# Decoder layer on one NeuronCore: the attention step's two transpositions, second diagonals and output projection in another order

## The chip, the core and the metric

One Trainium2 chip, one NeuronCore. The metric is device time in microseconds (us) of one execution of the whole kernel; lower is better. TensorE (PE, with its weight loads as PEld), VectorE (DVE), ScalarE (ACT), GpSimd (POOL) and SyncE (SP, which issues the DMAs) each run a stream of their own, in order, and meet at semaphores.

## The reference, cut

Four sequences of 512 tokens, width 512. A gated slot attention of 16 heads (key 64, value 128, 64 slots), a grouped-query cross attention without weights, and a ternary-like feed-forward of 1408, each followed by a residual add and a layernorm. The change lies in the first part alone:

```python
q, k, v = heads(x @ Wq, 64), heads(x @ Wk, 64), heads(x @ Wv, 128)
s = clip(heads(x @ Ws, 64), -32, 32)
z = cumlogsumexp(s);  p = exp(s - z);  g = exp(z_before - z)
hk = hk * g + k p^T;   ok = q/8 . hk          # scan over tokens, first pass
pv = softmax(ok)                              # over the 64 slots
hv = hv * g + p v^T;   o = pv . hv            # scan over tokens, second pass
gate = x @ Wg
o = o * rsqrt(mean(o^2) + eps) * g_norm_weight * silu(gate)
x = layernorm(x + o @ Wo)
```

## The kernel before

Attention runs in 32 steps (NSTEP), one for each pair of heads (8 pairs, `p`) and each sequence (4, `j`): step `n` = 4p + j. Both scans are done in chunks of 64 tokens (CHUNKS = 8): inside a chunk by a masked product ("diagonal"), across chunks by running sums of the chunks' states. Every projection is made with three matmuls for one (`mm3`, L61 to L63: low by high, high by low, high by high, in fp32r), for precision.

A step does the second half of pair-and-sequence n and the projections for n + 1, and is software pipelined by hand: the order of the calls in each engine's `step` is the order in which that engine works. The calls that matter here, on PE, in their order before the change:

- `key_scores` (L1202), the projections S and K of step n + 1 (12 x 2 matmuls of 512 columns), `key_states` (L1218), `slots` (L1271), `states` (L1239), `slots_from_states` (L1282).
- projection V0 (VG in the code: v and gate of 128 tokens, 12 matmuls), then **the slots' transposition** (`transpose4(okb, ... okn ...)`, L1129) which waits for okn_ready.
- V1, V2, then **the weights' transposition** (`transpose4(tb, ... pv ...)`, L1129 as well), which waits for pv_ready.
- V3, then wT_ready, the **second diagonals** (`diagonals`, L1228) and `values_from_states` (L1295).
- projection Q, the output projection of step n - 1 (`project_out`, four tiles of 6 matmuls, L61 to L63 with a_wo in their names), and `values` (L1305).

Up to step 28 (`LATE_OUT`) the output projection stands there; in the last three steps it stands elsewhere, and these keep their order. Step 0 has no output projection, so 28 steps (1 to 28) do.

The output projection's four tiles use two PSUM banks (`out_banks`: okb and tb, tile t in bank t % 2). Tile 2 waits until DVE has added tile 0 to acc, tile 3 until tile 1 is added (`wait(pe, added, 4 * (n - 1) + t - 1)` in `project_out`). The adds are `add_out` on DVE (L1968), each behind its tile (`wo_done`).

The two projection banks `pj` alternate: a projection waits until the one two before it has been read, V and gate groups by `gating` on DVE (L1880), which follows the copy of v (L1642) and the tanh (L1644) on ACT.

DVE's order around the change, before: `gating` V0, `slot_maxima` (L1989), `less_maxima` (L1994), `gating` V1, `slot_sum` (L2000), `scaled_weights` (L2004, waits for the weights' transposition and gives wT), `gating` V2, `slot_reciprocals` (L2008), `running_z` (L1888, a scan of the next step's exponentials into rz, which must not overwrite rz before `scaled_weights` has read it), `low_turned` (L1960), `mask_diagonal_blocks` (L1917, waits for the second diagonals and for ACT's `rows_of_keys`), `gating` V3, `inverse_z` (L1894 and L1895, two reciprocals of 128 x 256), the four adds, `gated_output` (L2017).

ACT's order: V0's copies, the exponential (L1710), V1's copies, `rows_of_e` (L1664, waits for a DMA), V2's copies, `high_turned` (L1658, waits for a DMA), `rows_of_keys` (L1670, waits for a DMA), V3's copies, the copy of Q (L1623), sums of squares (L1686).

SP sends e, the outputs and the keys to DRAM in 32-row blocks and fetches them back turned (`put_e`, `put_og`, `put_keys`, `get_e`, `get_og`, `get_keys`), then loads weights. POOL does the norm's factor and the splits of weights. Neither has a changed line.

Of the kernel before, what the change touches and what calls it, by code (L numbers as in the profile page):

```python
# [142 lines left out]
def layer_program(nc, x, ctx_in, Wq, Wk, Wv, Wg, Ws, Wo, gw, gate_w, up_w, down_w, gate_s, up_s, down_s, out,  # L143
# [6 lines left out]
    with ExitStack() as ctx:  # L150
# [10 lines left out]
        def sem(name):  # L161
            return ctx.enter_context(nc.semaphore("a_" + name))
# [102 lines left out]
        ok_done = sem("ok_done")  # L265
        pvT_done = sem("pvT_done")
        o_done = sem("o_done")
        e_done = sem("e_done")

        queries_kept = sem("queries_kept")  # L270
# [61 lines left out]
        def at(n, k):  # L332

            return isinstance(n, int) and n == k
# [714 lines left out]
        def _(pe):  # L1049
# [237 lines left out]
            def values_from_states(n):  # L1287

                ob = value_banks(n)
                if LATE_OUT < n < NSTEP - 1:  # L1290
                    pe.wait_ge(added, 4 * n)
                for c in range(1, CHUNKS):
                    i, r = c // 2, c % 2
                    for h in range(2):
                        pe.matmul(ob[h][HALF[r ^ h], i * P:(i + 1) * P], wT[HALF[h], c * CHUNK:(c + 1) * CHUNK],  # L1295
                                  state[HALF[h], c - 1, :], start=(c == 1 or c == 2), stop=False, skip_group_check=True)

            def values(n, j):

# [20 lines left out]
            def step(n, p, j, first):  # L1320
                b1, pair1 = (j + 1) % B, p if j < B - 1 else p + 1

                def next_project(*groups):
                    for i in groups:
                        project(n + 1, i, b1, pair1)

                into = n == NSTEP - 2
                key_scores(n)
                next_project(S, K)
                key_states(n)  # L1330
                slots(n)
                states(n, j)
                slots_from_states(n)
                next_project(VG)
                pe.wait_ge(okn_ready, n + 1)
                transpose4(okb, [okn[:, t * P:(t + 1) * P] for t in range(TT)]).then_inc(ok_done, 1)
                pair0 = p if j else p - 1
                if at(n, 0):
                    pe.wait_ge(state_ready, CHUNKS - 1)
                    transpose_x(2, range(KT))  # L1340
                if at(n, 1):
                    transpose_x(3, (0, 1))
                next_project(VG + 1)
                if into:
                    transpose_operands(0, 0, 0)
                    transpose_operands(0, 0, 1)
                next_project(VG + 2)
                if into:
                    pe.wait_ge(opsT_ready, 1)
                    transpose_operands(0, 0, 2)  # L1350
                pe.wait_ge(pv_ready, n + 1)
                pe.wait_ge(state_ready, (CHUNKS - 1) * (n + 1))
                transpose4(tb, [pv[:, 2 * t:2 * t + 2, :].rearrange("p h m -> p (h m)") for t in range(TT)])\
                    .then_inc(pvT_done, 1)
                if at(n, 1):
                    transpose_x(3, (2, 3))
                if into:
                    pe.wait_ge(opsT_ready, 2)
                    transpose_operands(0, 0, 3)
                next_project(VG + 3)  # L1360
                if into:
                    pe.wait_ge(opsT_ready, 3)
                    transpose_operands(0, 0, 4)
                    pe.wait_ge(wT_ready, n + 1)
                    max_pair(0, 0)
                if n > LATE_OUT:
                    project_out(n, pair0, (0, 1))
                    if into:
                        max_pair(0, 1)
                    project_out(n, pair0, (2, 3))  # L1370
                pe.wait_ge(wT_ready, n + 1)
                if at(n, 0) or at(n, 1):
                    pe.wait_ge(xlo_ready, (n + 3) * KT)
                if into:
                    pe.wait_ge(opsT_ready, TILES)
                    max_pair(0, 2)
                diagonals(n)
                values_from_states(n)
                if into:
                    max_pair(0, 3)  # L1380
                next_project(Q)
                if not first and n <= LATE_OUT:
                    project_out(n, pair0, (0, 1, 2, 3))
                if into:
                    max_pair(0, 4)
                pe.wait_ge(proj_done, PROJ * (n + 2))
                values(n, j)
# [200 lines left out]
        def _(act):  # L1588
# [109 lines left out]
            def step(n, p, j, first):  # L1698
                b1 = (j + 1) % B

                def next_proj(*groups):
                    for i in groups:
                        copy_proj(n + 1, i, b1)

                if not first:
                    square_sums(n - 1, 0)
                into = n == NSTEP - 2
                next_proj(S, K, VG)
                act.wait_ge(sub_ready, n + 1)
                nc.scalar.activation(pv, pv, ACT.Exp, scale=QK_SCALE).then_inc(pv_ready, 1)  # L1710
                if at(n, 0):
                    high_x(2)
                if at(n, 1):
                    high_x(3, (0, 1))
                next_proj(VG + 1)
                if into:
                    copy_keys(0, 0)
                    copy_queries(0, 0, 1)
                rows_of_e(n + 1)
                next_proj(VG + 2)  # L1720
                if at(n, 1):
                    high_x(3, (2, 3))
                if into:
                    copy_queries(0, 0, 2)
                    copy_queries(0, 0, 3)
                if not first:
                    high_turned(n)
                rows_of_keys(n + 1)
                next_proj(VG + 3)
                if into:  # L1730
                    copy_queries(0, 0, 4)
                next_proj(Q)
                square_sums(n, 1)
                place_sums(n)
# [97 lines left out]
        def _(dve):  # L1832
# [189 lines left out]
            def step(n, p, j, first):  # L2022
                b1 = (j + 1) % B
                norm_now = at(p, PAIRS - 1) and j > 0
                into = n == NSTEP - 2
                late = n <= LATE_OUT
                mask_scores(n)
                if not first:
                    gated_output(n - 1, (j - 1) % B, 1)
                clip(n + 1, b1)  # L2030
                turn_e(n + 1)
                running_key_states(n)
                if not first:
                    turn_output(n)
                normalised_slots(n)
                turn_keys(n + 1)
                running_states(n)
                gating(n + 1, VG, b1)
                slot_maxima(n)
                less_maxima(n)  # L2040
                if at(n, 0):
                    low_x(2)
                if at(n, 1):
                    low_x(3, (0, 1))
                gating(n + 1, VG + 1, b1)
                slot_sum(n)
                scaled_weights(n)
                gating(n + 1, VG + 2, b1)
                slot_reciprocals(n)
                if at(n, 1):  # L2050
                    low_x(3, (2, 3))
                running_z(n + 1)
                if not first:
                    low_turned(n)
                if late:
                    mask_diagonal_blocks(n)
                gating(n + 1, VG + 3, b1)
                if into:
                    reduce_max(0, 0, 0)
                if not first and not late:  # L2060
                    add_out(n, (j - 1) % B, (0, 1))
                if into:
                    reduce_max(0, 0, 1)
                if not first and not late:
                    add_out(n, (j - 1) % B, (2, 3))
                if into:
                    reduce_max(0, 0, 2)
                if not late:
                    mask_diagonal_blocks(n)
                if norm_now and not into:  # L2070
                    statistics(n, j - 1)
                if into:
                    reduce_max(0, 0, 3)
                    reduce_max(0, 0, 4)
                if norm_now and not into:
                    norm.apply(dve, j - 1, j - 1, j - 1)
                inverse_z(n + 1)
                if not first and late:
                    add_out(n, (j - 1) % B, (0, 1, 2, 3))
                gated_output(n, j, 0)  # L2080
# [245 lines left out]
```

## Time and profile before

| what | value |
|---|---|
| median of 3 runs | 1848.08 us (1846.91 to 1848.42) |
| the profiled execution's own time | 1847.07 us |
| its span on the core | 1845.0 us |
| attention's steps 2 to 28 begin | 94.66 to 925.50 us |
| PE busy | 1806.2 us, 98% |
| DVE busy | 1346.9 us, 73% |
| ACT busy | 734.9 us, 40% |
| POOL busy | 571.9 us, 31% |

The page gives busy shares over the whole span, and in 40 slices. PE's matmuls are pipelined, so its records overlap; how long a stretch takes is read best from the start of one group of matmuls to the start of the next. A view by windows gives busy time and the granted clock of a stretch; the view of waits says who waited for whom; the timeline lists instructions by their start, with the idle time before one and what ended it in square brackets.

### The profile page before, as it was taken

The numbers are of one execution on the slowest core, as the hardware profiler recorded it, in microseconds if no ns is written. First come the engines' busy times: TensorE is split into PE (matmuls) and PEld (weight loads), VectorE is DVE, ScalarE is ACT, GpSimd is POOL, SyncE is SP. The second block draws the span as 40 slices with busy tenths as digits, with TensorE's granted clock in tenths as the row PEclk, the third lists the DMA queues.
The fourth block names the chain that finished last, engine by engine and source line by source line (L and its number), as shares of the span: only waits on it lengthen the run. The fifth ranks groups of instructions, "written<-read, shape, count | busy, mean of one in ns | idle before, by whom it ended". The sixth has DMA issues, their size and how long they took to land.

```text
span 1845.0 us, 39065 instructions
## 1 busy us (share of the span) xinstructions
PE 1806.2 (98%) x15728; PEld 1327.9 (72%) x15728; DVE 1346.9 (73%) x2459; ACT 734.9 (40%) x1853; POOL 571.9 (31%) x595
## 2 busy tenths in 40 slices
PE   9999999999999999999998899999999999999998
PEld 7888888888888888888886654444434488888886
DVE  4777677777777677677776789999999665555556
ACT  3323332322323332223322238888888722222223
POOL 3050341333332412503322242444423133323322
PEclk9999999999999999999998889999999999999999
DMA  4324232422333142323212101111111211111112
GB/s 155 97 57 117 68 111 59 110 81 70 87 90 101 51 123 64 92 82 87 81 47 60 44 20 28 26 25 28 28 29 22 28 17 31 22 26 27 18 18 91
DMA packets 191267, 111.63 MB, mean 61 GB/s; under 512 B 96624, under 2 KB 170864, under 8 KB 191088
## 3 DMA queue, kind: packets, MB, share of 16 engines
q1 hardware_dynamic: 191088, 109.14, 22.6%
q8 instruction: 125, 2.05, 0.5%
q14 instruction: 54, 0.44, 0.1%
HBM read 64.77 MB, written 36.18 MB: 55 GB/s over the span
## 4 chain that ended last, share of the span: by engine, by line
PE 91%; DVE 3%; ACT 3%; POOL 1%; issue 1%; DMA 0%; SPq 0%; POOLq 0%; DVEq 0%; ACTq 0%
PE a_ps L61 21%; PE a_ps L63 20%; PE a_ps L62 20%; PE a_ps L1113 6%; PE a_ps L1075 5%; PE a_ps L1097 3%; PE a_ps L1129 2%; PE a_ps L1057 2%; ACT x_prob L1774 2%; PE a_ps L1305 2%; PE a_ps L1282 1%; PE a_ps L1239 1%; PE a_ps L1295 1%; PE a_ps L1228 1%; PE a_ps L1120 1%; DVE a_raw_qks L1838 1%
## 5 line engine op out<-in xcount | busy, mean ns | idle before, releaser
L1838 DVE TENSOR_REDUCE a_raw_qks<-a_ps 128x1 f32<-128x512 f32 x512 | 320.8, 681 | 19.2 <-PE a_ps L1075 18.5
L1774 ACT ACTIVATE x_prob<-a_ps 128x512 f32<-128x512 f32 x512 | 280.0, 608 | 62.9 <-PE a_ps L1097 61.4
L61 PE MATMUL a_ps<-a_vg_hi,a_xT_lo 128*128 128x512 f32 x512 | 209.2, 409 | 0.0
L63 PE MATMUL a_ps<-a_vg_hi,a_xT_hi 128*128 128x512 f32 x512 | 200.7, 392 | 0.0
L62 PE MATMUL a_ps<-a_vg_lo,a_xT_hi 128*128 128x512 f32 x512 | 199.5, 390 | 0.0
L893 POOL TENSOR_TENSOR a_f<-a_rs 128x8 f32<-128x8 f32 x32 | 6.4, 201 | 606.4 <-ACT a_flat L1686 606.4
L61 PE MATMUL a_ps<-a_xT_hi,a_qks_lo 128*128 128x512 f32 x384 | 157.1, 409 | 0.4 <-DVE a_xT_lo L1869 0.4
L1968 DVE TENSOR_TENSOR acc<-acc,a_ps 128x512 f32<-128x512 f32 x128 | 87.8, 687 | 89.1 <-PE a_ps L63 88.6
L62 PE MATMUL a_ps<-a_xT_lo,a_qks_hi 128*128 128x512 f32 x384 | 150.7, 392 | 0.0
L63 PE MATMUL a_ps<-a_xT_hi,a_qks_hi 128*128 128x512 f32 x384 | 149.9, 390 | 0.0
L1075 PE MATMUL a_ps<-a_xT_lo,a_xT_hi 64*128 64x512 f32 x384 | 143.3, 462 | 3.1 <-DVE a_raw_qks L1838 2.5
L1097 PE MATMUL a_ps<-a_xT_hi,a_xT_lo 64*128 64x512 f32 x384 | 140.8, 452 | 0.6 <-ACT x_prob L1774 0.5
L1686 ACT ACTIVATE a_flat<-a_ps 128x128 bf16<-128x128 f32 x256 | 67.4, 278 | 182.2 <-PE a_ps L1305 174.8
L61 PE MATMUL a_ps<-a_xT_hi,f_gu_lo 128*128 128x512 f32 x352 | 137.4, 390 | 0.8 <-POOL f_gu_lo L992 0.8
L1113 PE MATMUL a_ps<-x_prob,x_values 128*32 128x512 f32 x1024 | 137.0, 608 | 0.0
L63 PE MATMUL a_ps<-a_xT_hi,f_gu_hi 128*128 128x512 f32 x352 | 137.0, 389 | 0.0
L62 PE MATMUL a_ps<-f_xT_lo,f_gu_hi 128*128 128x512 f32 x352 | 137.0, 389 | 0.0
L1075 PEld LDWEIGHTS a_ps<-a_xT_lo,a_xT_hi 64*128 64x128 f32 x384 | 61.1, 188 | 98.5 <-issue 39.6
L1642 ACT COPY a_v<-a_ps 128x256 f32<-128x256 f32 x128 | 47.1, 368 | 201.2 <-PE a_ps L63 201.0
L2197 DVE TENSOR_TENSOR acc<-acc,a_ps 128x512 f32<-128x512 f32 x172 | 114.0, 684 | 0.0
L63 PEld LDWEIGHTS a_ps<-a_vg_hi,a_xT_hi 128*128 128x128 f32 x512 | 96.1, 188 | 21.5
L61 PE MATMUL a_ps<-a_wo_hi,a_oT_lo 128*128 128x512 f32 x256 | 101.8, 398 | 8.6 <-DVE a_oT_lo L1960 7.0
(201 smaller groups left out, 4055.0 us busy)
## 6 DMA issues: line engine op xcount, KB each, us to landing
a_og_blocks<-a_og_turn SPq DMA_DIRECT2D x120, 128.0 KB, 2.4
a_og_turn<-a_og_blocks SPq DMA_DIRECT2D x30, 512.0 KB, 4.0
a_e_blocks<-a_e_turn SPq DMA_DIRECT2D x124, 64.0 KB, 1.8
a_key_blocks<-a_causal SPq DMA_DIRECT2D x124, 64.0 KB, 1.8
a_e_turn<-a_e_blocks SPq DMA_DIRECT2D x31, 256.0 KB, 2.9
a_causal<-a_key_blocks SPq DMA_DIRECT2D x31, 256.0 KB, 4.1
a_raw_vg<-in_L_attn_Wv_dram SPq DMA_DIRECT2D x8, 512.0 KB, 6.7
a_raw_vg<-in_L_attn_Wg_dram SPq DMA_DIRECT2D x8, 512.0 KB, 7.8
```

The lines of the kernel that those rows point to most:

```text
L61: pe.matmul(out, w_lo, x_hi, start=start, stop=False)
L62: pe.matmul(out, w_hi, x_lo, start=False, stop=False)
L63: return pe.matmul(out, w_hi, x_hi, start=False, stop=stop)
L1075: pe.matmul(max_bank(u, q, i, par), qs[q][HALF[par], tile, st * P:(st + 1) * P], ks[q][(tile // 2) ^ par][HALF[par], :], start=True, stop= ...
L1097: pe.matmul(score_bank(q, s, par), ks[q][g ^ par][HALF[par], t * P:(t + 1) * P], qs[q][HALF[par], 2 * g + pair, :], start=True, stop=True) ...
L1113: mm = pe.matmul(avb[32 * i:32 * (i + 1), :], cv[:, q, t, g, :], prob[i % 2][:, (s + i // 2) % 4, :], start=(t == 0), stop=(t == TT - 1))
L1642: nc.scalar.copy(v[:, b % 2, i - VG, :], bank[:, 0:2 * DV]).then_inc(v_ready, 1)
L1686: sq = nc.scalar.activation(squares[:, g, 0:DV], ob[half][:, t * P:(t + 1) * P], ACT.Square, scale=DV ** -0.5, accum_out=crossed_sums[:, t ...
L1774: nc.scalar.activation(prob[par][:, s % 4, :], score_bank(q, s, par), ACT.Exp, scale=X_SCALE).then_inc(exp_done[par], 1)
L1838: nc.vector.tensor_reduce(nm[:, q % 2, i % 4, par, i // 4:i // 4 + 1], max_bank(u, q, i, par), AX.X, ALU.max, negate=True).then_inc(max_re ...
L1968: nc.vector.tensor_tensor(a, a, out_banks(n)[t % 2], ALU.add).then_inc(added, 1)
L2197: nc.vector.tensor_tensor(a, a, down_bank(t), ALU.add).then_inc(f_added, 1)
```

## The change

In the steps up to LATE_OUT:

- PE: V1 is put in front of the slots' transposition, and V3 in front of the weights' transposition. Q goes in front of the second diagonals and `values_from_states`, so that these stand right in front of the output projection.
- PE: in front of `values`, the wait for the projections' end becomes a wait for the output projection's first tile (step 0: for a new semaphore vals_started, which `values_from_states` raises).
- PE, steps 0 and 1: the transpositions of x and the wait for xlo_ready move along.
- ACT: V1's copies go in front of the exponential. For all steps, the copies of x of step 1 (tiles 2 and 3) go behind V3's.
- DVE: `gating` V1 goes in front of `slot_maxima`; `low_turned` directly behind `gating` V2 (in all steps); `gating` V3 and then `scaled_weights` behind it; `running_z` and `mask_diagonal_blocks` follow. `slot_reciprocals` stands behind `slot_sum` in all steps. `inverse_z` and the adds keep their place behind all that.

```diff
@@ PE @@
                 for c in range(1, CHUNKS):
                     i, r = c // 2, c % 2
                     for h in range(2):
-                        pe.matmul(ob[h][HALF[r ^ h], i * P:(i + 1) * P], wT[HALF[h], c * CHUNK:(c + 1) * CHUNK],
-                                  state[HALF[h], c - 1, :], start=(c == 1 or c == 2), stop=False, skip_group_check=True)
+                        mm = pe.matmul(ob[h][HALF[r ^ h], i * P:(i + 1) * P], wT[HALF[h], c * CHUNK:(c + 1) * CHUNK],
+                                       state[HALF[h], c - 1, :], start=(c == 1 or c == 2), stop=False,
+                                       skip_group_check=True)
+                if n == 0:
+                    mm.then_inc(vals_started, 1)
...
                 slots_from_states(n)
+                pair0 = p if j else p - 1
+                if n <= LATE_OUT:
+                    next_project(VG, VG + 1)
+                    pe.wait_ge(okn_ready, n + 1)
+                    transpose4(okb, [okn[:, t * P:(t + 1) * P] for t in range(TT)]).then_inc(ok_done, 1)
+                    if at(n, 0):
+                        pe.wait_ge(state_ready, CHUNKS - 1)
+                        transpose_x(2, range(KT))
+                    if at(n, 1):
+                        transpose_x(3, (0, 1))
+                    next_project(VG + 2, VG + 3)
+                    pe.wait_ge(pv_ready, n + 1)
+                    pe.wait_ge(state_ready, (CHUNKS - 1) * (n + 1))
+                    transpose4(tb, [pv[:, 2 * t:2 * t + 2, :].rearrange("p h m -> p (h m)") for t in range(TT)])\
+                        .then_inc(pvT_done, 1)
+                    if at(n, 1):
+                        transpose_x(3, (2, 3))
+                    next_project(Q)
+                    pe.wait_ge(wT_ready, n + 1)
+                    if at(n, 0) or at(n, 1):
+                        pe.wait_ge(xlo_ready, (n + 3) * KT)
+                    diagonals(n)
+                    values_from_states(n)
+                    if not first:
+                        project_out(n, pair0, (0, 1, 2, 3))
+                        pe.wait_ge(wo_done, 4 * (n - 1) + 1)
+                    else:
+                        pe.wait_ge(vals_started, 1)
+                    values(n, j)
+                    return
                 next_project(VG)
                 pe.wait_ge(okn_ready, n + 1)
...
                 next_project(Q)
-                if not first and n <= LATE_OUT:
-                    project_out(n, pair0, (0, 1, 2, 3))
                 if into:
@@ ACT @@
                 next_proj(S, K, VG)
+                if n <= LATE_OUT:
+                    next_proj(VG + 1)
                 act.wait_ge(sub_ready, n + 1)
                 nc.scalar.activation(pv, pv, ACT.Exp, scale=QK_SCALE).then_inc(pv_ready, 1)
...
-                next_proj(VG + 1)
+                if n > LATE_OUT:
+                    next_proj(VG + 1)
...
                 next_proj(VG + 2)
-                if at(n, 1):
-                    high_x(3, (2, 3))
...
                 next_proj(VG + 3)
+                if at(n, 1):
+                    high_x(3, (2, 3))
@@ DVE @@
                 gating(n + 1, VG, b1)
+                if late:
+                    gating(n + 1, VG + 1, b1)
                 slot_maxima(n)
                 less_maxima(n)
...
-                gating(n + 1, VG + 1, b1)
+                if not late:
+                    gating(n + 1, VG + 1, b1)
                 slot_sum(n)
-                scaled_weights(n)
+                slot_reciprocals(n)
+                if not late:
+                    scaled_weights(n)
                 gating(n + 1, VG + 2, b1)
-                slot_reciprocals(n)
+                if not first:
+                    low_turned(n)
+                if late:
+                    gating(n + 1, VG + 3, b1)
+                    scaled_weights(n)
                 if at(n, 1):
                     low_x(3, (2, 3))
                 running_z(n + 1)
-                if not first:
-                    low_turned(n)
                 if late:
                     mask_diagonal_blocks(n)
-                gating(n + 1, VG + 3, b1)
+                if not late:
+                    gating(n + 1, VG + 3, b1)
```

## Rows read from the trace of the kernel before

**Rows 1.** The page: PE's granted clock in 40 slices of the span, in tenths.

```profile
PEclk9999999999999999999998889999999999999999
```

**Rows 2.** Windows, steps 2 to 27: PE, PEld, DVE, ACT, POOL busy (count), clock, DMA share, GB/s.

```profile
94.66:925.50 830.84, 830.84 (x9264) 683.85 (x9260) 598.38 (x1118) 253.82 (x858) 258.50 (x230) 1.00 0.30 85
```

**Rows 3.** Waits, 94.66 to 925.5 us: who waited for whom, us in total, times, longest.

```profile
ACT a_key_rows L1670 <- DMA a_causal<-a_key_blocks: 3.8, 7, 1.1
```

**Rows 4.** Timeline of PE, step 11: start, length, engine, line, operation, form, count, idle before.

```profile
391.34 0.50 PE L61 MATMUL a_ps<-a_vg_hi,a_xT_lo 128*128 128x512 f32 x1
...
394.20 0.60 PE L1129 MATMUL a_ps<-ident,a_flat 128*128 128x128 f32 x4
...
400.13 0.60 PE L1129 MATMUL a_ps<-ident,a_flat 128*128 128x128 f32 x4
...
403.41 0.69 PE L1228 MATMUL a_ps<-a_flat,a_eT 64*64 64x64 f32 x32
...
404.90 0.50 PE L61 MATMUL a_ps<-a_xT_hi,a_qks_lo 128*128 128x512 f32 x1
...
407.80 0.39 PE L61 MATMUL a_ps<-a_wo_hi,a_oT_lo 128*128 128x512 f32 x1
...
413.33 1.10 PE L1305 MATMUL a_ps<-a_v,a_causal 64*64 64x128 f32 x32
```

**Rows 5.** Timeline of DVE, step 11.

```profile
400.77 0.69 DVE L2004 TENSOR_TENSOR a_flat<-a_ps,a_rz 128x512 f32<-128x512 f32 x1 [1.37 <-PE a_ps L1129]
...
401.82 1.17 DVE L1888 TENSOR_TENSOR_SCAN a_rz<-a_eT 128x512 f32<-128x512 f32 x1
...
404.32 0.76 DVE L1917 TENSOR_TENSOR a_causal<-a_ps,a_mask 128x256 f32<-128x256 f32 x2 [0.22 <-ACT a_key_rows L1670]
404.99 0.41 DVE L1880 SCALAR_TENSOR_TENSOR a_gate<-a_gate,a_ps 128x256 f32<-128x256 f32 x1
405.32 1.75 DVE L1894 RECIPROCAL a_rz<-a_rz 128x256 f32<-128x256 f32 x1
406.98 1.70 DVE L1895 RECIPROCAL a_rz<-a_rz 128x256 f32<-128x256 f32 x1
409.36 0.69 DVE L1968 TENSOR_TENSOR acc<-acc,a_ps 128x512 f32<-128x512 f32 x1 [0.68 <-PE a_ps L63]
```

**Rows 6.** Timeline of ACT, step 11.

```profile
403.60 0.62 ACT L1670 COPY a_key_rows<-a_causal 128x512 f32<-128x512 f32 x1 [1.07 <-DMA a_causal<-a_key_blocks]
404.13 0.37 ACT L1642 COPY a_v<-a_ps 128x256 f32<-128x256 f32 x1
404.39 0.39 ACT L1644 ACTIVATE a_gate<-a_ps 128x256 f32<-128x256 f32 x1
```

**Rows 7.** Timeline of PE, step 16: the second diagonals.

```profile
563.17 0.69 PE L1228 MATMUL a_ps<-a_flat,a_eT 64*64 64x64 f32 x32
```

**Rows 8.** Timeline of DVE, step 16: the mask behind these diagonals.

```profile
563.94 0.76 DVE L1917 TENSOR_TENSOR a_causal<-a_ps,a_mask 128x256 f32<-128x256 f32 x2
```

**Rows 9.** Timeline of PE, step 31: an output tile that waited for an add.

```profile
1068.64 0.47 PE L61 MATMUL a_ps<-a_wo_hi,a_oT_lo 128*128 128x512 f32 x1 [0.31 <-DVE acc L1968]
1068.95 0.40 PE L62 MATMUL a_ps<-a_wo_lo,a_oT_hi 128*128 128x512 f32 x1
```

**Rows 10.** Timeline of DVE, step 31: the adds that it waited for.

```profile
1067.81 1.29 DVE L1968 TENSOR_TENSOR acc<-acc,a_ps 128x512 f32<-128x512 f32 x2
```

**Rows 11.** Timeline of PE, step 29: the first matmuls behind a long wait.

```profile
985.64 0.77 PE L61 MATMUL a_ps<-a_wo_hi,a_oT_lo 128*128 128x512 f32 x1 [7.01 <-DVE a_oT_lo L1960]
986.21 0.63 PE L62 MATMUL a_ps<-a_wo_lo,a_oT_hi 128*128 128x512 f32 x1
```

**Rows 12.** Windows around that wait, columns as in rows 2.

```profile
975.00:991.00 16.00, 8.99 (x31) 6.89 (x31) 4.54 (x7) 3.30 (x7) 0.00 (x0) 0.70 0.42 119
```

**Rows 13.** Timeline of PE, step 0: the slots' transposition, then that of x.

```profile
44.10 0.60 PE L1129 MATMUL a_ps<-ident,a_flat 128*128 128x128 f32 x4
44.83 1.97 PE L1129 MATMUL a_ps<-ident,acc 128*128 128x128 f32 x16
```

More of the change, by code:

```diff
@@ L267, in layer_program @@
         o_done = sem("o_done")
+        vals_started = sem("vals_started")
         e_done = sem("e_done")
@@ L1336, in step @@
                 transpose4(okb, [okn[:, t * P:(t + 1) * P] for t in range(TT)]).then_inc(ok_done, 1)
[L1337 to L1340, printed above, removed]
-                if at(n, 1):
-                    transpose_x(3, (0, 1))
                 next_project(VG + 1)
@@ L1354, in step @@
                     .then_inc(pvT_done, 1)
-                if at(n, 1):
-                    transpose_x(3, (2, 3))
                 if into:
@@ L1371, in step @@
                 pe.wait_ge(wT_ready, n + 1)
-                if at(n, 0) or at(n, 1):
-                    pe.wait_ge(xlo_ready, (n + 3) * KT)
                 if into:
@@ L1720, in step @@
                 next_proj(VG + 2)
-                if at(n, 1):
-                    high_x(3, (2, 3))
                 if into:
```

## Prediction

> **What bounds the kernel now.** I read the page first: the granted clock is full nearly throughout [rows 1], so time is matmuls and gaps on PE. Then the windows of the steady stretch, steps 2 to 27: 830.84 us for 26 steps, 31.96 us each, with PE busy in all of it [rows 2]. The view of waits of the same stretch has no line in which PE waits for DVE, ACT, POOL or a DMA; the one DMA wait that the change comes near is ACT's for the turned keys, 3.8 us over 7 steps [rows 3]. So the steady steps hold no data wait that an order could remove. The third view, PE's timeline of one step, gives what each group takes from its start to the next one's start [rows 4]: V0 2.86 us (391.34 to 394.20); a transposition with the 24 matmuls behind it 5.93 us (394.20 to 400.13); the weights' transposition and V3 3.28 us; the second diagonals with values_from_states 1.49 us (403.41 to 404.90); Q 2.90 us; the output projection 5.53 us (407.80 to 413.33), so that one tile takes about 1.37 us. Last I read DVE's and ACT's timelines of that step, since the change may turn their slack into waits.
>
> **PE's own work.** No matmul is added or removed. What could change is the cost at borders between kinds. Before, a step crosses from V to transposition and back twice, from 128-row to 64-row work twice (V3 to diagonals, output to values), and back once (values_from_states to Q). After, it does the same: V1 and V3 meet the transpositions, Q meets the diagonals, values_from_states meets the output projection. I take 0. The bounds are a tenth either way: the first matmul behind 64-row work takes 0.50 us, one in the dense stream 0.39 us [rows 4], and one such step more or less is 0.11 us a step, 3 us in 28.
>
> **The transpositions' new places.** The slots' transposition comes one group later (V1, some 2.7 us, half of the 24 matmuls in [rows 4]), the weights' one group later too, so two groups lie between them as before. In front of the weights' transposition DVE now does one gating, about 0.33 us (404.99 to 405.32 [rows 5]), before the maxima, and ACT's exponential follows; the two groups' cover of some 5.6 us stays far above these four operations of 0.4 to 0.7 us. I cost it at nothing; without cover it would be 0.33 us a step.
>
> **Q in front of the diagonals.** The weights' transposition now starts where V3 has ended, and Q's 2.9 us lie between it and the diagonals, as V3's did. In that time DVE must gate V3 (behind ACT's v copy and tanh), then make wT. With the transposition at T, V3's last matmul, 0.39 us long and begun 0.23 us ahead of T, ends at T + 0.2; V3's copy starts there at best, tanh 0.26 us later for 0.39 us [rows 6]: gating at about T + 0.9, scaled_weights 0.33 us behind, 0.69 us long [rows 5], wT at T + 1.9. The diagonals come at T + 3.3. The margin is 1.4 us, smaller when ACT is held by the turned keys. Step 11 is such a step: the key copy starts at 403.60, 12.26 us behind V0's start at 391.34 [rows 4, 6]. From there 0.53 us to V3's copy, 0.26 to the tanh, 0.39 to its end [rows 6], 0.33 to scaled_weights, 0.69 to wT [rows 5]: 2.20 us, 14.46 us behind V0's start. The diagonals in the new order come 2.86 + 2.72 (V0, V1) + 5.93 (transposition, V2, V3) + 3.28 (transposition, Q for V3) = 14.79 us behind it [rows 4]. Just in time. Cost 0; once late, it is one for one.
>
> **What is late next: the adds.** This is the term that decides. Call the start of the diagonals D.
>
> PE: 1.49 us for diagonals and values_from_states, then the output projection starts; its tiles 0 and 1 are 12 matmuls behind 64-row work, as Q is now, 2.90 us [rows 4]. Tile 2 would start at D + 4.39. It may start only when DVE has added tile 0.
>
> DVE: the mask can't start before the diagonals are done. Where nothing else held it, it started at D + 0.77 (563.17 to 563.94 [rows 7, 8]). running_z in front of it is done by then: in a usual step wT is ready at T + 1.9 = D - 1.4, and the scan takes 1.17 us [rows 5]. From the mask to the next operation 0.67 us (404.32 to 404.99), the first reciprocal 1.66 us to the start of the second (405.32 to 406.98), the second 1.70 us less the 0.08 us by which DVE's records overlap (404.99 + 0.41 against 405.32), 1.62 us, and the add 0.69 us [rows 5]. Sum: 0.77 + 0.67 + 1.66 + 1.62 + 0.69 = D + 5.41 us.
>
> In the kernel before, Q stood between: the output began at D + 4.39, tile 2 at about D + 7.1, and DVE was free at 408.7 and itself waited 0.68 us for tile 0 [rows 5]. Now the 2.9 us of Q are gone from that place while the two reciprocals, 3.3 us, stay in front of the add. A wait of PE for just this add exists in the trace, at the end of attention: the first add ended at 1067.81 + 0.69 = 1068.50 [rows 10], the tile started at 1068.64, 0.14 us later, and its second matmul followed after 0.31 us where the dense spacing is 0.23 us [rows 9]: 0.08 us more.
>
> So tile 2 starts at D + 5.41 + 0.14 = 5.55 instead of D + 4.39: 1.16 us, with the restart 1.24 us a step. Tile 3 waits for the add of tile 1, 0.7 us later, and tile 2 takes 1.37 us: no second wait. values waits for the mask, long done, and for its own engine's tile 0. Behind the waiting tile on PE stand tiles 2 and 3, values and the whole next step, so the wait is paid in full. Bounds: without latency and restart, and with the DVE chain 0.05 us shorter, 0.97 us; with the restart at 0.11 us and no overlap of DVE records, 1.35 us. I take 1.24 us, since each part of it has its own row: times 28 steps, 34.7 us (27.2 to 37.8).
>
> **Steps 0 and 1, and the rest.** In step 0 the slots' transposition took 0.73 us to the next group, where a steady one takes about 0.36 us (3.28 less 12 matmuls' 2.9) [rows 4, 13]: it waited for the running states, which are ready now: -0.4 us. Step 0 has no output projection, so its values wait for the mask (D + 0.77 + 0.75 = D + 1.52 against D + 1.49): 0.1 to 0.2 us, as much as the wait that it loses. The transpositions of x are as many as before. In steps 29 and later only low_turned and the tiny reciprocal are earlier; in step 29 PE waits 7.01 us for low_turned [rows 11], but that ends with a DMA and ACT's copy, not with running_z: 0. The new waits on PE for its own groups are met when reached. The DMAs are issued by SP in the same order, from turns that DVE makes in front of all that is changed: 0. POOL's splits start a little earlier against the projections: 0.
>
> **Sum.** 34.7 - 0.4 = +34.3 us. On the profiled execution's 1847.07 us that is 1881.4 us; the median of the runs shown lies 1.0 us above that execution, so 1882.4 us for the median.
>
> **Rivals.**
>
> - *The adds don't hold PE, and the order is neutral.* For it: DVE is busy only 72% of the steady stretch [rows 2], and before the change the adds waited for PE. Against it: the chain mask, reciprocals, add is in order on one engine and 1 us longer than PE's path. Time: 1847.7 us as a median. The same result follows if the change doesn't lengthen the steady steps for a reason that I don't see.
> - *Faster: the borders shrink.* PE's only gaps in a steady step are those at changes of kind. If diagonals that come behind Q, or an output behind 64-row work, save one restart of 0.11 us a step, and PE's stream hides the adds as in the case above, the time is 1848.1 - 0.4 - 28 x 0.11 = 1844.6 us. It needs an add that is in time, which decides from D + 4.3 us. One restart more instead gives 1850.8.
> - *The keys bind too.* If the turned keys land later than in step 11 in most steps, DVE's gating of V3, wT and the mask move one for one, and PE stands in front of the diagonals as well. 0.3 us a step more is 8 us: 1890 us. For it: the margin there is 0.3 us in step 11. Against it: ACT waited for the keys in 7 of 26 steps only [rows 3], and their DMAs hang on earlier work.
> - *The clock falls.* Behind the 7.01 us wait of step 29, a matmul took 0.63 us in place of 0.39 us, and the stretch's mean clock was 0.70 [rows 11, 12]: 1.2 GHz for a while. If each step's new wait did that for some 10 us, which would cost 5 us, the time would be 1882 + 28 x 5 = 2022 us. Against it: only long waits did so here, and PE is dense on both sides of a wait of 1.2 us. The Trainium skill ("TensorE: Matmul & The Clock Gate", "A second HAM failure mode: psum-queue depth-cycling") says that cycling through PSUM banks with short idle moments between groups of matmuls can make the clock swing between its levels; this is such a pattern, one idle moment a step at a bank's hand-over. By the same page's section on oscillation the fall is paid anew in each turn of the loop. By that rule the clock rival holds; no row of the steady stretch shows such a fall, as there is no wait in it.
>
> **How the numbers follow.** Forecast (PE waits for the first add in each of 28 steps) 0.82; neutral 0.08; faster 0.03; keys bind too 0.05; clock 0.02. The predicted time is 1882.4 us. Its own bounds are 1875 (27.2 us) to 1886 us (37.8 us); toward the rival with the keys I go to 1889 us. 1875 to 1889 us then holds some 8 in 10. About 0.2%, 3.7 us, is what a measurement of this kernel can tell from no change: faster 0.03 (1844.6 and less), same 0.08, slower 0.89.
>
> **What would show it.** In the changed kernel's view of waits, a line in which PE's L61 waits for DVE acc (L1968), 28 times, 1.1 us each, some 31 us in all; steady steps of 33.2 us in place of 31.96; on DVE the reciprocals directly in front of the first add, and no idle time before that add. If PE instead waits at the diagonals for a_flat (L2004), the keys rival holds; if the clock of 94 to 960 us is under 1.00, the clock rival. If the steps keep 31.96 us, my DVE chain is wrong, and the first thing to look at would be the start of the mask against D.

## The result, and the profile after

| kernel | median | span profiled | ratio to before, 95% interval |
|---|---|---|---|
| before | 1847.49 us | 1845.0 us | |
| after | 1879.39 us (1879.1 to 1883.48) | 1877.0 us | 1.0179 (1.0166 to 1.0191) |

The change costs 31.9 us (1879.39 - 1847.49). The forecast was 1882.4 us, in a range from 1875 to 1889 us.

The page of the changed kernel, PE's granted clock in 40 slices, in tenths, which answers to [rows 1]:

```profile
PEclk9999999999999999999998999999999999999999
```

Windows over the same 26 steps (2 to 27), columns as in [rows 2]:

```profile
96.04:956.76 860.72, 838.92 (x9265) 681.86 (x9260) 610.57 (x1118) 250.86 (x858) 263.60 (x230) 1.00 0.29 82
```

860.72 us for 26 steps is 33.10 us each, against 31.96 us before: 1.15 us more (29.88 us over 26 steps). DVE is busy for much the same time (610.6 us, 598.4 us before), the clock is 1.00, and PE, which was busy throughout, now lacks 21.8 us. The view of waits over steps 2 to 27 names where (who for whom, us in total, times, longest):

```profile
PEld a_ps L61 <- DVE acc L1993: 32.9, 26, 1.3
PE a_ps L61 <- DVE acc L1993: 21.8, 26, 0.8
```

One wait a step, for the add (L1968 has become L1993), and no other wait of PE for data in that stretch. The two rows are one wait seen twice: the record of the weight load ends before that of the matmul in front of it. PE's idle time is 0.84 us each time, less than a step's loss of 1.15 us, because a matmul's record lasts 0.39 us where a dense one follows after 0.23 us: the delay of a tile is read from start to start. The timeline of PE in step 11 shows the place:

```profile
402.97 0.50 PE L61 MATMUL a_ps<-a_vg_hi,a_xT_lo 128*128 128x512 f32 x1
...
408.56 0.60 PE L1130 MATMUL a_ps<-ident,a_flat 128*128 128x128 f32 x4
...
414.49 0.60 PE L1130 MATMUL a_ps<-ident,a_flat 128*128 128x128 f32 x4
...
417.76 0.69 PE L1229 MATMUL a_ps<-a_flat,a_eT 64*64 64x64 f32 x32
418.28 1.05 PE L1296 MATMUL a_ps<-a_state,a_flat 64*64 64x128 f32 x28
419.26 0.50 PE L61 MATMUL a_ps<-a_wo_hi,a_oT_lo 128*128 128x512 f32 x1
...
421.92 0.39 PE L63 MATMUL a_ps<-a_wo_hi,a_oT_hi 128*128 128x512 f32 x1
423.15 0.50 PE L61 MATMUL a_ps<-a_wo_hi,a_oT_lo 128*128 128x512 f32 x1 [0.84 <-DVE acc L1993]
423.49 0.40 PE L62 MATMUL a_ps<-a_wo_lo,a_oT_hi 128*128 128x512 f32 x1
...
426.14 1.10 PE L1309 MATMUL a_ps<-a_v,a_causal 64*64 64x128 f32 x32
```

The row at 421.92 is the last matmul of tile 1, that at 423.15 the first of tile 2. From V0's start to the diagonals everything is dense (14.79 us, as worked out from [rows 4]); between the two rows PE stands: 1.23 us from start to start, where the dense spacing is 0.23 us. And DVE in the same step, which answers to [rows 5]:

```profile
415.38 0.42 DVE L1905 SCALAR_TENSOR_TENSOR a_gate<-a_gate,a_ps 128x256 f32<-128x256 f32 x1 [0.21 <-ACT a_gate L1666]
415.71 0.68 DVE L2029 TENSOR_TENSOR a_flat<-a_ps,a_rz 128x512 f32<-128x512 f32 x1
416.50 1.22 DVE L1913 TENSOR_TENSOR_SCAN a_rz<-a_eT 128x512 f32<-128x512 f32 x1
418.52 0.75 DVE L1942 TENSOR_TENSOR a_causal<-a_ps,a_mask 128x256 f32<-128x256 f32 x2 [0.80 <-PE a_ps L1229]
419.20 1.74 DVE L1919 RECIPROCAL a_rz<-a_rz 128x256 f32<-128x256 f32 x1
420.86 1.69 DVE L1920 RECIPROCAL a_rz<-a_rz 128x256 f32<-128x256 f32 x1
422.47 1.22 DVE L1993 TENSOR_TENSOR acc<-acc,a_ps 128x512 f32<-128x512 f32 x2
```

In [rows 5] the add at 409.36 had waited 0.68 us for PE, and the reciprocals had been over before. Now it has no idle time in front of it, and two adds stand back to back (x2): the roles have changed, PE waits for DVE. A chain as short as this shows up on the page too, as 3% of the span for each reciprocal in the chain of work that ended last; neither stands among its lines before.

### The profile page after: what moved, and what is told of

It reads as the page before. It is cut to its first block, busy times and chain, and to the rows that moved or that the text cites. A ratio compares the mean times of both kernels' runs of the same rounds, so it can differ in the third digit from the quotient of the medians.

```text
span 1877.0 us, 39065 instructions
## 1 busy us (share of the span) xinstructions
PE 1814.4 (97%) x15728; PEld 1325.8 (71%) x15728; DVE 1359.7 (72%) x2459; ACT 731.6 (39%) x1853; POOL 576.5 (31%) x595
## 4 chain that ended last, share of the span: by engine, by line
PE 85%; DVE 10%; ACT 3%; POOL 1%; issue 1%; DMA 1%; SPq 0%; POOLq 0%; DVEq 0%; ACTq 0%
PE a_ps L61 20%; PE a_ps L63 19%; PE a_ps L62 18%; PE a_ps L1114 6%; PE a_ps L1076 5%; PE a_ps L1098 3%; DVE a_rz L1919 3%; DVE a_rz L1920 3%; PE a_ps L1130 2%; PE a_ps L1058 2%; ACT x_prob L1799 2%; PE a_ps L1309 2%; PE a_ps L1283 1%; PE a_ps L1240 1%; DVE a_causal L1942 1%; PE a_ps L1229 1%
## 5 line engine op out<-in xcount | busy, mean ns | idle before, releaser
L61 PE MATMUL a_ps<-a_wo_hi,a_oT_lo 128*128 128x512 f32 x256 | 108.7, 425 | 32.2 <-DVE acc L1993 23.8
L1993 DVE TENSOR_TENSOR acc<-acc,a_ps 128x512 f32<-128x512 f32 x128 | 83.4, 670 | 60.6 <-PE a_ps L63 60.3
L1905 DVE SCALAR_TENSOR_TENSOR a_gate<-a_gate,a_ps 128x256 f32<-128x256 f32 x128 | 53.5, 418 | 86.6 <-ACT a_gate L1666 83.0
L2230 DVE TENSOR_TENSOR acc<-acc,a_ps 128x512 f32<-128x512 f32 x172 | 114.0, 684 | 0.0
```

The costliest lines, as they stand in the source:

```text
L61: pe.matmul(out, w_lo, x_hi, start=start, stop=False)
L1993: nc.vector.tensor_tensor(a, a, out_banks(n)[t % 2], ALU.add).then_inc(added, 1)
L2230: nc.vector.tensor_tensor(a, a, down_bank(t), ALU.add).then_inc(f_added, 1)
```

## The experiments

The theory: with Q gone from between the diagonals and the output projection, the chain mask, two reciprocals, first add on DVE is 1 us longer than PE's way to tile 2, which needs tile 0's bank. Rivals: PE's new order costs at its borders; wT or the turned keys hold PE; DVE's order delays something else.

**e1: the adds between the reciprocals.** DVE's order alone is altered (`inverse_z` now also takes which half to invert; its definition is left out here):

```diff
-                inverse_z(n + 1)
                 if not first and late:
-                    add_out(n, (j - 1) % B, (0, 1, 2, 3))
+                    inverse_z(n + 1, (0,))
+                    add_out(n, (j - 1) % B, (0, 1))
+                    inverse_z(n + 1, (1,))
+                    add_out(n, (j - 1) % B, (2, 3))
+                else:
+                    inverse_z(n + 1)
...
```

> The changed kernel with DVE's order alone altered in steps 1 to 28: first reciprocal, adds of tiles 0 and 1, second reciprocal, adds of tiles 2 and 3. If the first add behind two reciprocals is what holds PE, the first add can start when tile 0 is done (some 3.2 us behind the diagonals' start D, against D + 4.7 in the changed kernel), is over at D + 3.9, and tile 2 starts unhindered at D + 4.4: steps of 31.95 us and 1847 us in all (28 x 1.15 = 32.2 us less than 1879.4). If the cost lies in PE's own new order (the output projection behind 64-row work, Q behind a transposition), PE's order is unchanged here and the time stays at 1879 us. If the weights or the turned keys held PE in front of the diagonals it would stay there too.

Measured: 1846.95 us, ratio to before 0.9993 (0.9984 to 1.0003). The steps 2 to 27 are back at 31.97 us in the mean (31.96 before). DVE around the adds, in a step whose diagonals start at 405.41:

```profile
406.17 0.76 DVE L1944 TENSOR_TENSOR a_causal<-a_ps,a_mask 128x256 f32<-128x256 f32 x2 [0.29 <-PE a_ps L1229]
406.84 1.74 DVE L1922 RECIPROCAL a_rz<-a_rz 128x256 f32<-128x256 f32 x1
408.61 0.69 DVE L1995 TENSOR_TENSOR acc<-acc,a_ps 128x512 f32<-128x512 f32 x1
410.00 0.69 DVE L1995 TENSOR_TENSOR acc<-acc,a_ps 128x512 f32<-128x512 f32 x1 [0.70 <-PE a_ps L63]
410.60 1.74 DVE L1922 RECIPROCAL a_rz<-a_rz 128x256 f32<-128x256 f32 x1
```

and PE's row of tile 2's first matmul, 4.39 us behind the diagonals' start, with no wait in front:

```profile
409.80 0.39 PE L61 MATMUL a_ps<-a_wo_hi,a_oT_lo 128*128 128x512 f32 x1
```

The first add is over at 409.30, half a microsecond before tile 2, and the second add waits for PE again. PE's order is that of the changed kernel to the last call, and the whole loss is gone: PE's borders carry none of it, nor do wT and the keys.

**e2: a third bank.** Here DVE's order is the changed kernel's, but tile 2 has a bank of its own, the projection bank that V3 has left:

```diff
-            return (okb, tb) if n <= LATE_OUT else ob
+            if n <= LATE_OUT:
+                return (okb, tb, pj[n % B % 2], okb)[t]
+            return ob[t % 2]
...
-                    if t >= 2:
+                    if t >= 2 and n > LATE_OUT:
                         wait(pe, added, 4 * (n - 1) + t - 1)
+                    if t == 2 and n <= LATE_OUT:
+                        pe.wait_ge(gate_ready, 4 * (n + 2))
+                    if t == 3 and n <= LATE_OUT:
+                        wait(pe, added, 4 * (n - 1) + 1)
...
                 key_scores(n)
+                if 1 < n <= LATE_OUT + 1:
+                    pe.wait_ge(added, 4 * (n - 2) + 3)
                 next_project(S, K)
```

> The changed kernel with DVE's order as it is, but the output projection's tile 2 in the projection bank that V3 has left, and tile 3 in okb, which is free once tile 0 is added; the next S waits until tile 2 is added. If the hand-over of a bank from tile 0 to tile 2 is the cost, tile 2 needs no add now, and tile 3 (at D + 5.8 at the earliest) comes behind the first add's end at D + 5.3: 1847 us, steps of 31.95 us, although the reciprocals still stand in front of the adds. If DVE's order as such costs the time (its late work delaying what the next step needs), or PE's own order does, it stays at 1879 us.

Measured: 1846.48 us, ratio 0.9994 (0.9984 to 1.0004). DVE is as late as in the changed kernel, with three adds in a row behind the reciprocals (the diagonals start at 404.64, so the first add is D + 4.70):

```profile
406.07 1.74 DVE L1927 RECIPROCAL a_rz<-a_rz 128x256 f32<-128x256 f32 x1
407.73 1.70 DVE L1928 RECIPROCAL a_rz<-a_rz 128x256 f32<-128x256 f32 x1
409.34 1.93 DVE L2001 TENSOR_TENSOR acc<-acc,a_ps 128x512 f32<-128x512 f32 x3
```

and PE's row of tile 2's first matmul, 4.38 us behind the diagonals' start, with no wait in front:

```profile
409.02 0.39 PE L61 MATMUL a_ps<-a_wo_hi,a_oT_lo 128*128 128x512 f32 x1
```

Its steps are 31.97 us. So late adds alone cost nothing; they cost only through the bank that tile 2 needs. e1 and e2 take the same wait away from its two ends.

**e3: one operation more in the chain.** Gating of V3 back behind the mask:

```diff
                 if late:
-                    gating(n + 1, VG + 3, b1)
                     scaled_weights(n)
...
                 if late:
                     mask_diagonal_blocks(n)
-                if not late:
-                    gating(n + 1, VG + 3, b1)
+                gating(n + 1, VG + 3, b1)
```

> The changed kernel with gating of V3 put back behind the mask, as it stood before the change: one DVE operation of 0.33 us more between D and the first add. If the chain mask, (gating), reciprocals, add holds PE, each of the 28 steps grows by 0.33 us: 9.2 us, 1888.6 us in all, steps of 33.43 us. If PE is held by wT or the keys, scaled_weights comes 0.33 us earlier here and the time falls, by up to 9 us to 1870 us. If the cost is PE's own order, it stays at 1879 us.

Measured: 1888.07 us, ratio 1.0217 (1.0204 to 1.0231), steps of 33.44 us: 0.34 us more than after, as the operation takes on DVE (421.85 to 422.18):

```profile
421.18 0.76 DVE L1942 TENSOR_TENSOR a_causal<-a_ps,a_mask 128x256 f32<-128x256 f32 x2 [1.38 <-PE a_ps L1229]
421.85 0.41 DVE L1905 SCALAR_TENSOR_TENSOR a_gate<-a_gate,a_ps 128x256 f32<-128x256 f32 x1
422.18 1.75 DVE L1919 RECIPROCAL a_rz<-a_rz 128x256 f32<-128x256 f32 x1
```

The wait follows its supposed cause one for one, and wT, which came earlier here, has no share.

**e4: Q's move alone**, in the kernel before:

```diff
+                if not first and n <= LATE_OUT:
+                    next_project(Q)
                 diagonals(n)
                 values_from_states(n)
...
-                next_project(Q)
+                if first or n > LATE_OUT:
+                    next_project(Q)
...
                 pe.wait_ge(proj_done, PROJ * (n + 2))
+                if not first and n <= LATE_OUT:
+                    pe.wait_ge(wo_done, 4 * (n - 1) + 1)
                 values(n, j)
```

> The kernel before the change with one part of it alone: in steps 1 to 28 Q goes in front of the second diagonals; both transpositions, ACT's and DVE's orders stay as before (on DVE gating of V3 stands between the mask and the reciprocals). If Q's departure from between the diagonals and the output projection makes the whole loss, this has it all and 0.33 us a step more: 33.43 us a step, 1847.5 + 28 x 1.48 = 1889 us. If the moved transpositions carry part of the loss, it is below 1879 us.

Measured: 1888.94 us, ratio 1.0223 (1.0209 to 1.0237), steps of 33.45 us against e3's 33.44 us. In both, gating of V3 stands between the mask and the reciprocals, and Q in front of the diagonals; they differ in where the two transpositions are and in the rest of DVE's and ACT's order. So Q's move alone is enough for the whole loss, and with Q there the places of the two transpositions are worth nothing in the steady steps. That they are worth nothing by themselves isn't shown by this: e5 keeps them and takes Q's move away. PE's wait is for the add here too (the view of waits over the whole kernel, with one such wait in step 31):

```profile
PE a_ps L61 <- DVE acc L1973: 33.1, 29, 1.2
```

The 0.9 us between the medians is near the 0.6 us of step 0, which e4 doesn't gain.

**e5: Q taken away from in front of the diagonals**, in the changed kernel, in steps 1 to 28:

```diff
-                    next_project(Q)
+                    if first:
+                        next_project(Q)
                     pe.wait_ge(wT_ready, n + 1)
...
                     values_from_states(n)
                     if not first:
+                        next_project(Q)
                         project_out(n, pair0, (0, 1, 2, 3))
```

> The changed kernel with Q put back between values_from_states and the output projection in steps 1 to 28, both transpositions in their new places: now nothing lies between the weights' transposition (start T) and the diagonals. This prices the cover that Q gives to wT. By the changed kernel's trace of step 12's predecessor, the transposition starts at 414.49, scaled_weights, behind the gating of V3, at 415.71 and is over at 416.39, so the diagonals start at 416.45, some 1.5 us later than PE could (414.84 and a border of 0.1); the adds are in time again, as Q's 2.9 us are back. Steps of about 33.45 us, 1847.3 - 0.6 + 28 x 1.5 = 1889 us. If wT is not on any path (the rival that the adds' wait is the only thing that the new order can run into), the time falls back to 1847 us.

Measured: 1886.78 us, ratio 1.0212 (1.0196 to 1.0227), steps of 33.34 us. PE in step 11:

```profile
417.65 0.60 PE L1130 MATMUL a_ps<-ident,a_flat 128*128 128x128 f32 x4
419.62 0.69 PE L1229 MATMUL a_ps<-a_flat,a_eT 64*64 64x64 f32 x32 [1.37 <-DVE a_flat L2031]
```

The adds are in time again, and wT is the wait in their place, of much the same size. The estimate was 1.5 us a step; measured were 1.38 us (33.34 against 31.96). With the weights' transposition behind V3, one projection has to cover wT and one the reciprocals, and only Q is left: either place alone loses. So the moved transpositions, with the orders of DVE and ACT that go with them, aren't free by themselves: without Q behind them they cost nearly as much as Q's move does.

**e6 and e7: the queue of SP in step 29.** The largest single wait of PE, 7.0 us before and 7.2 us after, is for low_turned in step 29. The change puts low_turned earlier on DVE there and leaves the wait as it is. e6 is e1 with this edit, e7 the kernel before with it:

```diff
-                if n == NSTEP - 3:
-                    sp.wait_ge(wo_ready, PAIRS)
-                    for q in range(2):
-                        get_rows(q, 0, q)
                 put_e(n + 1)
...
                 get_keys(n + 1)
+                if n == NSTEP - 3:
+                    sp.wait_ge(wo_ready, PAIRS)
+                    for q in range(2):
+                        get_rows(q, 0, q)
```

> e1 (adds between the reciprocals) with one more edit on SP: in step 29 the wait for the last output weights and the two loads that follow it go behind the six block moves of that step, in front of which they stood. In the kernel before, these moves are issued 14 us late there, and PE waits 7.0 us for low_turned and then runs 24 matmuls of the output projection in 8.1 us instead of 5.5 us at the lower clock. If SP's queue is the cause, the 7 us wait and the slow matmuls go: step 29 takes some 33 us in place of 42.4 us, 1838 us in all. If the DMAs themselves or POOL's late work hold the step, little changes: 1845 to 1847 us.

> The kernel before the change with e6's edit on SP alone. It tells whether e6's gain of 9 us needs the new order. If the gain is SP's queue in step 29 and nothing else, this gains the same: 1847.4 - 9.1 + the 0.6 us of step 0 = 1838.5 to 1839 us. If the new order (low_turned in front of the running sum in the last steps) is part of it, since low_turned now decides in step 29, it stays some tenths to 1.1 us behind e6: up to 1840 us.

Measured: e6 1838.39 us, ratio 0.9948 (0.9936 to 0.9961); e7 1838.82 us, ratio 0.9954 (0.9940 to 0.9967). The SP timeline of the kernel before, in step 29, which begins at 957.45:

```profile
971.58 0.93 SPq L678 DMA_DIRECT2D a_raw_qks<-in_ctx_dram  x2
972.62 1.88 SPq L619 DMA_DIRECT2D a_e_blocks<-a_e_turn  x4
```

and of e6, whose step 29 begins at 957.71:

```profile
963.53 1.79 SPq L620 DMA_DIRECT2D a_e_blocks<-a_e_turn  x4
```

The block moves no longer stand behind a wait for POOL's last weights; they start 9.3 us earlier in the step (5.8 us behind its start, as in step 28; that is how late they were, not the 14 us of the expectation). PE's wait for low_turned is 0.44 us there in place of the 7.01 us of [rows 11], and the output projection behind it runs at full clock:

```profile
979.34 0.47 PE L61 MATMUL a_ps<-a_wo_hi,a_oT_lo 128*128 128x512 f32 x1 [0.44 <-DVE a_oT_lo L1987]
```

Step 29 takes 33.15 us in place of 42.44 us. This is the fastest version of the study, 9 us below the kernel before. The medians of e6 and e7 are 0.4 us apart and their runs overlap, so nearly all of the gain is SP's. The traces do show a part of the new order that the medians don't. Without it, e7's PE still waits for low_turned in step 29:

```profile
PE a_ps L61 <- DVE a_oT_lo L1960: 1.3, 1, 1.3
```

and that step takes 33.95 us, 0.8 us more than e6's. With the 0.6 us of step 0 that makes 1.4 us in e6's favour. In the profiled executions it is made up for by the stretch ahead of step 0, which no edit touches and which took 32.70 us in e6 and 31.82 us in e7, and by 0.6 us more behind step 29 in e6, whose cause stays open.

## Why the prediction was right

**The mechanism, point by point.** PE waits for the first add in each of 28 steps, as forecast: shown by the waits, and by e1 and e2, which each remove it from another end. The sign named in advance, some 31 us in all and 1.1 us each, has to be read from start to start: the delay of tile 2 is 1.00 us, and the view of waits counts 0.84 us of it as idle. PE's own borders were put at 0: e1's steps with the new order take 31.97 us, 31.96 us before. The transpositions' new places were put at nothing: in the changed kernel the maxima come behind the gating of V1 and no wait of PE follows; e3 and e4, with the new places and the old, agree to 0.01 us a step. The cover of wT was put at a margin of 1.4 us: wT is over at 416.39 and the diagonals start at 417.76, 1.37 us later. That e5, with the cover gone, loses 1.38 us a step is another quantity, and the likeness is chance: there the diagonals start 1.97 us behind the transposition (417.65 to 419.62), just when wT is ready. The keys didn't bind in any step: PE has no wait for a_flat in the stretch.

**The sum.** The DVE chain was D + 5.41; it is 422.47 + 0.63 - 417.76 = D + 5.34 (0.63 us is the record of the first add; the two records of the pair overlap by 0.08 us, so it isn't half of 1.22 us). The parts up to the add fit to 0.01 us: 0.76 to the mask, 0.68, 1.66 and 1.61 us to the add's start at D + 4.71. What was mis-sized is the add with its hand-over. From the add's start to tile 2's, the rows of step 31 gave 0.69 + 0.14 = 0.83 us [rows 9, 10]; here it is 0.68 us (422.47 to 423.15), of which 0.06 us lie behind the end of the add's record, not 0.14 us. Tile 2 starts at D + 5.39 instead of the forecast D + 5.55, a wait of 1.00 us against e1's D + 4.39. In the other direction the restart costs 0.15 us, not 0.08: the second matmul follows after 0.34 us instead of 0.31 us, and the next spacings are a little above the dense one, so that tiles 2 and 3 take 2.96 us up to `values` where they take 2.81 us in e1 (means of the steps). Together 1.15 us a step in place of 1.24 us, two errors of opposite sign: over 28 steps 32.2 us (from step 1's start at 61.17 to step 29's at 989.89, 928.72 us, against 896.51 us before) in place of 34.7 us. That is 2.5 us of the 3.0 us by which the forecast was high. The median before also came out 0.6 us lower than the 1848.08 us from which the forecast started.

**Step 0** gained 0.59 us (28.78 to 28.19 us) in place of 0.4 us. The slots' transposition keeps PE for 0.44 us in place of 0.73 us [rows 13]. I had left out that Q loses the borders on both of its sides there, since step 0 has no output projection to take them over: Q took 3.12 us between values_from_states and `values` (56.90 to 60.02), and a projection in a dense stream takes 2.72 us, 0.40 us less (the wait of `values` for Q's end, which the forecast did count, included). The wait for the mask costs 0.17 us, as worked out.

**The rivals.** Neutral and faster fall with the waits. The clock didn't fall: 1.00 over all 26 steps with one wait of 1 us in each, at the hand-over of a bank. The Trainium skill ("TensorE: Matmul & The Clock Gate", "A second HAM failure mode: psum-queue depth-cycling") tells of a kernel in which short idle moments between groups of matmuls were frequent enough for the clock to swing; this trace shows no swing with one such moment in 33 us, and the measurement decides. It fell, as before, behind the 7 us wait of step 29 (0.88 in the mean over that step in both kernels), and not in e6 (1.00), where that wait is 0.44 us.

**The remainder.** The profiled spans differ by 32.0 us: 32.2 from steps 1 to 28, -0.6 from step 0, 0.8 from the start of the kernel up to step 0 (32.16 to 32.98 us), which the change doesn't touch (in the other runs it took from 31.14 us in e2 to 33.28 us in e5), and -0.4 behind step 28.

## What to carry to other kernels

Before work is moved away from between a producer and its consumer on a full engine, look at which chain on another engine it was covering, and add that chain up in that engine's own order: here Q would look free to move, since no row showed a wait, and it was hiding two reciprocals. A chain that ends in a buffer's release can be cut at either end, by doing the release first or by one more buffer, and an engine that is busy only 71% of the time can still be the one that is late. In the steady steps, whose trace showed no wait, none of the orders tried won anything, and four of them (after, e3, e4 and e5) lost 1.15 to 1.5 us a step; the gain of 9 us lay in the one long wait that the trace did show.

## What the runs showed of the hardware

- The hand-over from an add on DVE to a matmul took 0.68 us from the add's start in the steady steps, in all 28 of them alike to 0.01 us, and 0.83 us in step 31, for the same operation and shape. The record of the add differs too: 0.63 us in the steady steps, where it begins 0.08 us before the reciprocal's record ends, 0.69 us in step 31, where the record in front has ended (1067.78). That is 0.06 us of the difference of 0.15 us; the other 0.08 us lie between the add's end and the matmul's start. What makes either was not tried.
- A clock that fell behind a wait of 7 us (0.88 in the mean over step 29, matmuls 0.43 us apart instead of 0.23 us) stayed at full (1.00) through 28 waits of 1.0 us (after) and 1.3 us (e3, e4), one in each 33 us.
- PE's restart behind such a wait costs 0.14 us over its first six matmuls (1.50 us instead of e1's 1.36 us), at full clock.
- On DVE a reciprocal of 128 x 256 in fp32 takes 1.66 us up to the start of the next operation (419.20 to 420.86), more than twice the 0.69 us of an add of 128 x 512.
